# Grouping the indirect DMAs of the first expert stage by fours, each group behind the landing of the one in front

## What is computed

```python
x = x + attn_a(layernorm(x))
x = x + ffn(layernorm(x))
x = x + attn_b(layernorm(x))
x = x + ffn(layernorm(x))

def ffn(x):      # 8 batches in the original, 4 x 1024 tokens here
    probs = softmax(x @ Wr)                     # 8 experts
    topk_probs, topk_experts = top_k(probs, 2)
    pos = place of each token among those of its expert, in order
    keep = pos < capacity                       # 160 slots for each expert
    buf[expert, pos] = x where keep             # 1280 slots for a batch
    y = relu(buf @ W1 + b1) @ W2 + b2           # expert by expert
    return sum over k of y[expert, pos] * keep * topk_probs
```

## Time and profile before

| | us |
|---|---|
| median of 3 timed runs | 1464.06 |
| the profiled execution, its span | 1486.9 |
| TensorE busy in the span | 1437.6 (97%) |
| VectorE busy | 1065.3 (72%) |
| ScalarE busy | 917.8 (62%) |
| GpSimd busy | 280.4 (19%) |

### The profile page before, as it was taken

The page is one execution under the profiler, slowest core; times in us unless marked ns, Lnnn a source line. Parts: engine busy times, 40 slices in busy tenths (PEclk is TensorE's granted clock), DMA queues, the critical chain, the costliest instruction groups (busy, mean ns, idle before and its releaser), DMA issues.

```text
span 1486.9 us, 43341 instructions
## 1 busy us (share of the span) xinstructions
PE 1437.6 (97%) x18426; PEld 1023.7 (69%) x18426; DVE 1065.3 (72%) x2172; ACT 917.8 (62%) x1727; POOL 280.4 (19%) x325
## 2 busy tenths in 40 slices
PE   7999789999999999999999999999999999999996
PEld 6988774566677675667777756577777565677486
DVE  6884037888666678886766788876666887787754
ACT  5774466666666666566666666666666666666542
POOL 4164613013210012130000120400001214000055
PEclk9999999999999999999999999999999999999999
DMA  8501221001110011010000110110101101101002
GB/s 223 196 20 53 68 65 39 22 23 46 30 29 16 16 42 32 23 48 16 17 16 16 41 32 22 35 33 17 30 16 39 32 23 34 34 16 30 1 19 58
DMA packets 44464, 58.30 MB, mean 39 GB/s; under 512 B 8231, under 2 KB 32656, under 8 KB 44144
## 3 DMA queue, kind: packets, MB, share of 16 engines
q1 hardware_dynamic: 35120, 38.27, 9.4%
q0 software_dynamic: 9152, 17.26, 4.4%
HBM read 22.14 MB, written 19.32 MB: 28 GB/s over the span
## 4 chain that ended last, share of the span: by engine, by line
PE 87%; DVE 5%; ACT 3%; issue 2%; another core or an unknown queue 2%; DMA 0%; DVEq 0%; ACTq 0%
PE bank L1153 29%; PE bank L1166 28%; PE bank L1076 6%; PE bank L1081 4%; PE bank L1090 4%; PE bank L412 2%; PE bank L446 2%; PE bank L1308 2%; PE bank L1304 2%; DVE nmx L1188 1%; PE bank L1265 1%; ACT hT L542 1%; PE bank L830 1%; DVE stats L1349 1%
## 5 line engine op out<-in xcount | busy, mean ns | idle before, releaser
L1197 ACT ACTIVATE prob<-bank,nmx 128x1024 f32<-128x1024 f32 x512 | 570.2, 1114 | 420.3 <-DVE nmx L1188 408.5
L1188 DVE TENSOR_REDUCE nmx<-bank 128x1 f32<-128x1024 f32 x512 | 626.2, 1223 | 200.2 <-PE bank L1153 182.3
L1166 PE MATMUL bank<-prob,vsc 64*64 64x512 f32 x4096 | 644.9, 590 | 1.9 <-DVE ctxT L1215 1.4
L1153 PE MATMUL bank<-q,k 64*64 64x512 f32 x2048 | 527.6, 591 | 3.1 <-ACT prob L1197 1.9
L1153 PE MATMUL bank<-q,ks 64*64 64x512 f32 x2048 | 526.3, 590 | 0.0
L1166 PEld LDWEIGHTS bank<-prob,vsc 64*64 64x64 f32 x4096 | 237.3, 133 | 119.4 <-issue 47.1
L1076 PE MATMUL bank<-xT,wqkv_sb 64*64 64x256 f32 (+1 forms) x1560 | 211.7, 434 | 0.0
L1153 PEld LDWEIGHTS bank<-q,ks 64*64 64x64 f32 x2048 | 139.1, 133 | 75.9 <-issue 21.0
L1760 POOL DMA_INDIRECT yg<-yslots,row_ring x64 | 64.9, 1014 | 609.2 <-PE bank L1153 579.8
L1153 PEld LDWEIGHTS bank<-q,k 64*64 64x64 f32 x2048 | 135.3, 133 | 37.6 <-issue 8.6
L1076 PEld LDWEIGHTS bank<-xT,wqkv_sb 64*64 64x64 f32 x1560 | 92.2, 133 | 86.6 <-issue 36.5
(11 more groups left out here) (270 smaller groups left out, 1628.6 us busy)
## 6 DMA issues: line engine op xcount, KB each, us to landing
ks<-k SPq DMA_DIRECT2D x62, 256.0 KB
yslots<-slots_sb SPq DMA_DIRECT2D x7, 640.0 KB, 3.6
slots_sb<-xslots SPq DMA_DIRECT2D x5, 640.0 KB, 4.5
xslots<-xhat_r POOLq DMA_DIRECT2D x5, 512.0 KB, 7.0
yslots<-xhat_r POOLq DMA_DIRECT2D x5, 512.0 KB, 12.3
w_sb<-in_w SPq DMA_DIRECT2D x1, 2048.0 KB, 9.2
wqkv_sb<-in_wqkv SPq DMA_DIRECT2D x1, 2048.0 KB, 19.0
xslots<-xhat_r,row_s POOLq DMA_INDIRECT x112
```

Source lines behind the costliest of these rows:

```text
L1153: ins = nc.tensor.matmul(bank[rows(c), SC[h][n], :], kk[r, cols(2 * j + c, HD)], qst[pi % 2][r, cols(n, HALF)], start=True, stop=True)
L1166: ins = nc.tensor.matmul(bank[rows(h), CX[n], :], vsc[s][rows(r), rows(h)], prob[g % 3][h][rows(r), cols(n, HALF)], start=(j == 0 and firs ...
L1188: nc.vector.tensor_reduce(nmx[:, 2 * s + h:2 * s + h + 1], bank[:, SC[h][0]:SC[h][0] + 2, :], mybir.AxisListType.XY, ALU.max, negate=True) ...
L1197: nc.scalar.activation(prob[g % 3][h][:].rearrange("p (n c) -> p n c", c=HALF), bank[:, SC[h][0]:SC[h][0] + 2, :], ACT.Exp, bias=nmx[:, 2 ...
```

## The change

- `scatter` takes the tiles of a batch in fours. Ahead of tiles 4, 8 and 12 it waits until all transfers of the batch so far have landed, on two semaphores for each batch (even and odd tiles).
- `gather` waits ahead of quarters 1, 2 and 3 for the landing of the quarter in front.
- All pacing by TensorE's work in these scatters and this gather is gone: `scatter_in_attention`, `scatter_in_next` and `beside_expert` are removed. The bias of row 3 stands between tiles 7 and 8 of scatter 1.
- m = 2 gets a row tile of its own, `row_s2`, so that its places don't wait for scatter 1. For m = 3 VectorE writes `row_s` itself, after waiting for scatter 1, and the copy on GpSimd and `f_plc` are gone.
- The places of m = 3 are counted on TensorE ahead of the experts of the first batch, and expert 2 (not 5) waits for `f_kept`; the wait for `f_kept` ahead of the slots of m = 2 goes.
- Waits on `f_sc` elsewhere become waits on the pair of the batch in question.

```diff
-        f_plc = sem("f_plc")
...
-        f_sc, f_ld, f_st, f_comb = (sem(n) for n in ("f_sc", "f_ld", "f_st", "f_comb"))
+        f_sc = {m: [sem(f"f_sc{m}{i}") for i in range(2)] for m in (1, 2, 3)}
+        f_ld, f_st, f_comb = (sem(n) for n in ("f_ld", "f_st", "f_comb"))
         f_ga = [sem("f_ga0"), sem("f_ga1")]
-        f_gq = [sem(f"f_gq{q}") for q in range(4)]
+        f_gq = [[sem(f"f_gq{q}{i}") for i in range(2)] for q in range(4)]
...
-                a.wait_ge(f_sc, 256)
+                for done in f_sc[1]:
+                    a.wait_ge(done, 128)
...
-                if e == 5 and m == 1:
+                if e == 2 and m == 1:
...
-                if e == 3:
-                    positions(pe, 3, POS_F)
                 if e == E - 1:
-                    pe.wait_ge(f_kept, 3)
                     slots_ahead_tensor(pe, 2, slots2, AHEAD[:2])
...
+        def rows_to(m):
+            return row_s2 if m == 2 else row_s
...
-            if m > 1:
-                p.wait_ge(f_sc, 256 * (m - 1))
-            nc.gpsimd.tensor_copy(row_s[:], skip[:]).then_inc(f_idx, 1)
+            nc.gpsimd.tensor_copy(rows_to(m)[:], skip[:]).then_inc(f_idx, 1)
...
-            nc.vector.tensor_tensor(skip[:], rowf[:], skip[:], ALU.add).then_inc(f_plc, 1)
+            for done in f_sc[1]:
+                v.wait_ge(done, 128)
+            nc.vector.tensor_tensor(rows_to(m)[:], rowf[:], skip[:], ALU.add).then_inc(f_idx, 1)
...
-                v.wait_ge(f_gq[q], 64)
+                for done in f_gq[q]:
+                    v.wait_ge(done, 32)
...
-                nc.gpsimd.indirect_dma_start(out=xslots[:, :], out_offset=bass.IndirectOffsetOnAxis(ap=row_s[:, k, t:t + 1], axis=0),
+                if c > 0 and c % 4 == 0:
+                    hold(p, f_sc[m][0], 16 * (c // 2))
+                    hold(p, f_sc[m][1], 16 * (c // 2))
+                nc.gpsimd.indirect_dma_start(out=xslots[:, :], out_offset=bass.IndirectOffsetOnAxis(ap=rows_to(m)[:, k, t:t + 1], axis=0),
                                              in_=route_rows(m - 1)[:, t, :], in_offset=None,
-                                             bounds_check=B * SLOTS - 1, oob_is_err=False).then_inc(f_sc, 16)
-
-        def scatter_in_attention(p, m, next_row=None):
...
-        def beside_expert(p, i):
-
-            hold(p, f_h, E + i + 1)
+                                             bounds_check=B * SLOTS - 1, oob_is_err=False).then_inc(f_sc[m][c % 2], 16)
+
+        FIRST = 8
...
-                    beside_expert(p, 11 + 2 * q + k)
                     for t in (2 * q, 2 * q + 1):
+                        if q > 0 and k == 0 and t % 2 == 0:
+                            for done in f_gq[q - 1]:
+                                hold(p, done, 32)
                         nc.gpsimd.indirect_dma_start(out=yg[:, k, t, :], out_offset=None, in_=yslots[:, :],
                                                      in_offset=bass.IndirectOffsetOnAxis(ap=row_g[:, k, t:t + 1], axis=0),
-                                                     bounds_check=B * SLOTS - 1, oob_is_err=False).then_inc(f_gq[q], 16)
+                                                     bounds_check=B * SLOTS - 1, oob_is_err=False).then_inc(f_gq[q][t % 2], 16)
...
-            hold(sp, f_sc, 256 * m)
+            for done in f_sc[m]:
+                hold(sp, done, 128)
...
-            scatter_in_attention(p, 1, 3)
-            scatter_in_next(p, 1)
+            hold(p, f_idx, 2)
+            scatter(p, 1, range(FIRST))
+            bias_gpsimd(p, 3)
+            scatter(p, 1, range(FIRST, 2 * T))
             place_gpsimd(p, step, 2)
-            scatter_in_attention(p, 2)
-            scatter(p, 2, [13, 14, 15])
-            p.wait_ge(f_plc, 1)
-            p.wait_ge(f_sc, 256 * 2)
-            nc.gpsimd.tensor_copy(row_s[:], skip[:]).then_inc(f_idx, 1)
+            hold(p, f_idx, 3)
+            scatter(p, 2, range(2 * T))
             hold(p, f_idx, 4)
-            for i in range(8):
-                beside_expert(p, 3 + i)
-                scatter(p, 3, [2 * i, 2 * i + 1])
+            scatter(p, 3, range(2 * T))
             gather(p, step, 1, 0)
...
+            positions(pe, 3, POS_F)
```

More of the change, by code:

```diff
@@ L354, in bass_hybrid @@
         row_s = sb("row_s", [P, 2, T], U32, stack=stage_f)
+        row_s2 = sb("row_s2", [P, 2, T], U32, stack=stage_f)
         slots_sb = sb("slots_sb", [P, ST, P], stack=stage_f)
@@ L1415, in f_norm_vector @@
                 else:
-                    v.wait_ge(f_sc, 256 * (B - 1))
+                    for done in f_sc[B - 1]:
+                        v.wait_ge(done, 128)
                 xhat_vector(v, c0, fb, xhat_r, piece - 5, g_xhat)
```

## The result

The changed kernel takes 1475.35 us (median of 4, 1472.5 to 1476.2) against 1463.4 for the kernel before (median of 4, 1461.79 to 1464.46): ratio 1.0078, 95% interval 1.0064 to 1.0092. It is 11.95 us slower; 1473.9 was forecast. The profiled execution spans 1473.3 us and took 1475.03, so 1.7 us lie around the span.

What follows compares the result with a forecast made beforehand. TensorE bounds the long attention stage; its start hangs on TensorE's experts and, 1.8 us apart, GpSimd's DMAs, then VectorE. Start 7.2 us later plus 2.6 for the clock gives +9.8: 1473.9 us, range 1457 to 1478 (own range 1468 to 1478).

Steps and rivals of the forecast that it cites:

- GpSimd's chain: GpSimd's 48 scatters and 16 gathers before the long stage: scatter 1 from 79.94, last gather issued at 191.4 us after the change.
- Rival (b): Landing waits between DMA groups are cheaper, restart at the plain 0.30: 7.8 us come back, 1464 us; chance 0.12.
- Rival (a): Stalls ahead of the long stage are real in timed runs too: 5.6 us faster, 1458.5 us; chance 0.22.
- Are the stalls in the timed runs?: Stalls from 111 to 219 us taken as almost wholly of the profiled execution; taking them out gives 18.4 us.
- the missing 22.8 us: Profiled span of 1486.9 against timed median of 1464.06 us: at least this much claimed absent when nobody records.
- The price of a boundary: Wait between groups of four on GpSimd: each of 12 boundaries costs 1.9 us (scatters) or 2.25 us (gathers).
- 191 to 194 us: Sign in the profile after: the last gather issued near this time.
- The clock: TensorE's clock drops behind its hole of some 9 us ahead of the long stage: 2.6 us lost, added once.
- Starts of the long stage: TensorE-bound attention stage, 219 to 1415 us in the profile: timed start 195.6 before, 202.8 after, 7.2 us later.
- The cover of the slot load: SP's load of slots3 goes at about 165.3, 2 us later than TensorE would like, still off the path.
- Early places: Batch 3's positions counted ahead of all experts: scatter 3 no longer waits for places, running from 138.1, not 143.2.

## Why the prediction was right, point by point

- **The sign and its reason.** Forecast slower by 9.8 us for bare waits on GpSimd's chain; measured 11.95. With the waits out the kernel is 17.6 us faster: shown. Rival (b), cheap waits, would have had gaps near 0.30 + 1.28 us for scatters; they are 2.1 to 2.9. Rival (a), real stalls, didn't hold in the comparison. On the third chip its premise holds, and its kernel before (long stage at 214.0, measured 212.34), but not its outcome: it had the change 5.6 us faster with the long stage at 205.8, and measured are 0.2 us and 210.81, with landings later than it reckoned (gaps up to 4.33 us, 2.55 counted).
- **Are the stalls in the timed runs?** The conclusion, no, was right for these chips, and it decided the sign. The cause given, that recording brings them, was wrong. Each timed run has a span of its own, 1.7 to 2.4 us below its time, on every chip; a span of 1486.9 belongs to an execution of about 1488.7, like those of the third chip (1484.46 to 1492.02), and not to one of 1464. The span did come out shorter than 1486.9 beside a longer time, as forecast, but by 13.6 us and not 5 to 8, since this profile is of an execution without stalls. The right reading of the missing 22.8 us was "the profile is of an execution in other circumstances", and the arithmetic from there would have been the same. The sign holds only for chips like those of the comparison: on the third one the change isn't slower. By "Runtime: NRT & Kernel Launch" of the Trainium skill, section "The ~15µs preamble/postamble breakdown", a profile's total lies above the reported time; here the span lies below it, in every run. That the block that writes records held the engines back, which "NOTIFIC — the notification-queue block" of the Trainium skill, section "7.1 Overflow: three behaviours, one of which stalls the engine", had made thinkable, no run here shows: profiles of the first two chips are without stalls.
- **The price of a boundary.** The gaps of eight of the nine scatter boundaries (the bias covers the ninth) sum to 18.6 us, 2.33 each (2.23 predicted); the gathers' mean is 2.51 (2.55 predicted). Groups of scatters come 6.95 to 7.72 us apart (7.04 forecast), groups of gathers 7.30 to 7.56 (7.45 forecast). The two parts were each off while their sum held: of the third quarter, last issued at 188.75, VectorE takes the answers at 191.66 (2.91 later, 2.60 counted), and GpSimd, behind the same landing, issues at 192.40 (0.74 after VectorE, 0.95 counted).
- **GpSimd's chain** was mis-sized by the small things. Predicted: scatter 1 at 79.94, last issue at 191.4. Measured: 81.63 and 196.29. It began 1.7 us later, and took 3.2 longer: the places of batch 2 took 5.56 us (108.65 to 114.21) and not 4.76, several issues 1.1 to 1.45 and not 0.97, two boundaries 2.88 and 2.75. The kernel before had the same late start, 82.47, but not the 3.2 us. So the last gather came 9.8 us later than in before (196.29 against 186.51), where I had 7.3 (191.4 against 184.1) and had named 191 to 194 us as a sign of being right.
- **The clock.** This term, 2.6 us, was too large, and made good for the one above. I charged it to after alone, since I had TensorE idle only there. The kernel before has its own hole of 2.50 us with the clock at 0.57. From the start of xhat to the long stage takes 5.20 us in before and 5.37 in after: 0.2 us between them, and 0.9 more behind the start (spans 11.1 apart, starts 10.16). The sum measured is 10.0 + 0.2 + 0.9 = 11.1; forecast 7.2 + 2.6.
- **Starts of the long stage.** Forecast 195.6 and 202.8, measured 199.82 and 209.98. Both late, for the start of scatter 1 and the slow clock in the hand-over (from the end of xhat 3.06 and 3.23 us, 1.55 counted), in after also for the 3.2 us of GpSimd's chain.
- **The cover of the slot load failed.** "2 us later than TensorE would like, still off the path": the load left at 170.26 and TensorE idled 4.75 us for it. In after xhat came 6.30 us later still, so it cost nothing; with the scatters' waits alone it was nearly the whole cost, with the slow clock behind it.
- **Early places.** The forecast's scatter 3 began 5.1 us earlier for them (138.1 against 143.2); alone they start it 4.5 earlier and are worth 3.95 us, all measured on chips without stalls.
- **Where the change leads.** Without stalls, the change minus its waits (1457.72), with groups of eight (1458.29) and the kernel before with early places (1458.94) all beat both kernels, the kernel before by 0.3%, and can't be told from one another. Which of them is best where stalls are real wasn't tried.

## What to carry to other kernels

A wait for landing between groups of DMAs costs the gap that the timeline shows (here 1.8 to 2.2 us net each), but only once the chain that holds it is the last to arrive: ask for each whether it falls into slack, and which of its consumers (a load, a norm) binds first. If a profile's span is longer than the timed runs, it describes other circumstances: take its durations, not its stalls, and profile the same kernel again before reasoning about a cause. A remedy for a stall must be measured where the stall exists and where it doesn't; here the whole change is worth nothing in the one place and costs 0.8% in the other. Before one guard against a stall (the pacing) is taken out, measure the kernel without it where the stall exists: there it was worth 31 us, and on the other chips nothing.

## What the runs showed of the hardware

- The same program took 1462.8 us on two chips and 1486.87 on a third, in all 23 runs. The difference shows as "remote" waits: an engine goes on 6 us late for TensorE's product while GpSimd issues indirect DMAs back to back. On the third chip the longest such wait, 12.98 us, fell into scatter 2 issued as one series of 16 (114.05 to 134.8, no gap above 0.31 us), and with groups of four there was none ahead of the long stage (0.78 us in the profile with filler transposes); behind it, where no group reaches, there were waits of 1.0 us in one profile and of 9.88 us in the other. TensorE itself issued single matmuls with gaps of up to 1.03 us while that series ran, for which the profile names no releaser. On the first chip the same series of 16 without waits (111.74 to 132.1) gave none. What differs between the chips is open.
- A slow landing also occurs by itself: one gather boundary took 4.33 us on the third chip where its neighbours took 2.50 and 2.68, in the next kernel the same one 5.76, and on the second chip a pair boundary of scatters took 4.79.
- Holes of 2.5 and 6.3 us in TensorE's work were each followed by the 1.2 GHz level (0.57 and 0.50 over 4 us); with transposes running through most of the hole, and idle for 0.95 us, it stayed at 2.4 GHz; where they ended 5.91 us too early it fell (0.50 over 4 us).
